# Graph network, third edge stage: inverse square roots for four batches together in place of eight, and every later step four iterations closer to the gathers

## The reference, cut to what matters

```python
row, col = (edge_index[0], edge_index[1])
msg_in = jnp.concatenate([x[row], edge_attr], axis=-1)
h = msg_in @ W1 + b1
h = jax.nn.gelu(_layernorm(h, g1, be1), approximate=False)
msg = h @ W2 + b2
agg = jax.ops.segment_sum(msg, col, num_segments=x.shape[0])
```

## Time and profile before

| what | value |
|---|---|
| median of 3 runs | 5689.45 us (5686.22 to 5690.82) |
| the profiled execution, its own time | 5686.47 us |
| its span, first to last instruction | 5684.7 us |
| DVE busy | 4391.6 us (77%) |
| PE busy | 4194.4 us (74%) |
| POOL busy | 4193.2 us (74%) |
| ACT busy | 3617.8 us (64%) |
| mean granted TensorE clock | 0.846 of full |
| third edge stage, first gather to the start of the next stage | 3679.09 to 4709.18 us |

### The profile page before, as it was taken

The page is one execution under the profiler, slowest core; times in us unless marked ns, Lnnn a source line. Parts: engine busy times, 40 slices in busy tenths (PEclk is TensorE's granted clock), DMA queues, the critical chain, the costliest instruction groups (busy, mean ns, idle before and its releaser), DMA issues.

```text
span 5684.7 us, 86448 instructions
## 1 busy us (share of the span) xinstructions
PE 4194.4 (74%) x23301; PEld 3144.9 (55%) x23378; DVE 4391.6 (77%) x13886; ACT 3617.8 (64%) x12260; POOL 4193.2 (74%) x3819
## 2 busy tenths in 40 slices
PE   4766666766666666675688888578888885999995
PEld 3666665666666656565455555345555554554553
DVE  5887878787878787785788888667777776777776
ACT  4776767676767676673577777356776763555552
POOL 4787887788878787786577777577777754777776
PEclk6877777777777777777899999779999997999997
DMA  8867676767676766664477666456666662555553
GB/s 258 176 161 191 162 177 161 175 163 177 162 177 161 175 163 168 168 162 83 136 200 199 196 199 197 135 179 214 213 209 210 212 186 70 160 155 160 159 159 107
DMA packets 629401, 977.07 MB, mean 172 GB/s; under 512 B 105688, under 2 KB 339026, under 8 KB 628642
## 3 DMA queue, kind: packets, MB, share of 16 engines
q1 hardware_dynamic: 394242, 616.02, 33.7%
q0 software_dynamic: 234656, 355.35, 29.6%
HBM read 668.28 MB, written 306.11 MB: 171 GB/s over the span
## 4 chain that ended last, share of the span: by engine, by line
POOL 52%; issue 22%; DMA 12%; PE 8%; DVE 5%; ACT 1%; POOLq 0%; SPq 0%; DVEq 0%; ACTq 0%
POOL arena L1539 28%; POOL tab L1185 12%; POOL arena L1203 10%; DMA tab<-arena 9%; DMA arena<-T,srcI 2%; POOL arena L1236 1%; PE PS L1702 1%; PE PS L2043 1%; PE PS L2021 1%; PE PS L1497 1%; POOL arena L1209 0%; PE PS L828 0%; PE PS L301 0%; PE PS L848 0%; DVE arena L1526 0%
## 5 line engine op out<-in xcount | busy, mean ns | idle before, releaser
L1539 POOL DMA_INDIRECT arena<-T,srcI x2112 | 2022.0, 957 | 779.4 <-issue 632.1
L1185 POOL DMA_INDIRECT tab<-arena x784 | 1243.2, 1586 | 282.4 <-issue 223.7
L1203 POOL DMA_INDIRECT arena<-T,srcI x784 | 789.5, 1007 | 285.4 <-issue 275.0
L1526 DVE TENSOR_TENSOR_SCAN arena<-arena,PS 128x512 f32<-128x512 bf16 x588 | 748.3, 1273 | 180.9 <-PE PS L2348 81.3
L1506 ACT ACTIVATE arena<-PS 128x512 f32<-128x512 f32 x588 | 347.8, 591 | 640.8 <-PE PS L1497 640.8
L867 PE MATMUL PS<-arena 128*128 128x128 f32 x1568 | 306.2, 356 | 542.1 <-ACT arena L1132 542.1
L1606 DVE TENSOR_SCALAR arena<-PS,nodeid 128x512 bf16<-128x512 f32 x908 | 627.0, 737 | 75.5 <-PE PS L1587 75.4
L867 PEld LDWEIGHTS PS<-arena 128*128 128x128 f32 x1568 | 263.5, 254 | 581.0 <-ACT arena L1132 581.0
L848 PE MATMUL PS<-We,arena 65*128 65x256 f32 x1568 | 510.0, 408 | 58.1 <-DVE arena L890 31.7
L1702 PE MATMUL PS<-arena 128*128 128x396 bf16 x2800 | 541.8, 351 | 8.3 <-DVE arena L1606 6.8
L2330 PE MATMUL PS<-arena 128*128 128x512 bf16 x2323 | 543.8, 381 | 4.2 <-issue 0.2
(11 more groups left out here) (301 smaller groups left out, 10643.6 us busy)
## 6 DMA issues: line engine op xcount, KB each, us to landing
H<-arena SPq DMA_DIRECT2D x784, 256.0 KB, 2.3
arena<-keepR SPq DMA_DIRECT2D x294, 256.0 KB, 5.3
arena<-sF SPq DMA_DIRECT2D x98, 512.0 KB, 6.2
arena<-wF SPq DMA_DIRECT2D x98, 512.0 KB, 7.1
arena<-dF SPq DMA_DIRECT2D x98, 512.0 KB, 8.6
arena<-T,srcI POOLq DMA_INDIRECT x2896, 3.2
arena<-in_ea64T SPq DMA_DIRECT2D x98, 256.0 KB
arena<-S SPq DMA_DIRECT2D x98, 256.0 KB
```

Of the source, the lines that this page charges most:

```text
L1185: e.indirect_dma_start(out=tabs[k % KT], out_offset=at_rows(iA[b % 10][:, c:c + 1]), in_=X2[b % 3][:, c, :], in_offset=None, compute_op=AL ...
L1203: e.indirect_dma_start(out=Gs[b % NR][:, c, :], out_offset=None, in_=T0, in_offset=at_rows(srcI[:, CB * b + c:CB * b + c + 1])).then_inc(g ...
L1526: ins = e.tensor_tensor_scan(s[b % n][:, h, :], kR[g % 6][:, h0:h0 + CB * P], src[h], s[(b - 1) % n][:, h, CB * P - 1:CB * P] if b else in ...
L1539: e.indirect_dma_start(out=dst[:, c, :], out_offset=None, in_=T_tab, in_offset=at_rows(srcI[:, CB * b + c:CB * b + c + 1])).then_inc(gs.of ...
```

## The change

The group of batches for which the chain is run shrinks from eight to four: the tiles `var`, `rst`, `root`, `nh_` and `na_` go from 32 to 16 columns, the chain runs 49 times in place of 25, and each has the same 13 instructions. Since a group is now full after four batches, all steps from D on move four iterations forward: D from offset 12 to 8, T and r from 13 to 9, W from 14 to 10, the scan from 15 to 11, B, the copy and the store from 16 to 12, and SP's load of flags from 8 to 4. The loops end after `NBAT + 12` iterations. The gathers, the ring of 14 buffers, C, t and sq keep their place.

```diff
-            C8 = 8 * CB
-            NQ8 = (NBAT + 7) // 8
+            CQ = 4 * CB
+            NQ4 = (NBAT + 3) // 4
...
-                for i in range(NBAT + 16):
+                for i in range(NBAT + 12):
...
-                    if 0 <= i - 8 < NBAT and i % 2 == 0:
-                        rows_load(e, i - 8, kR, keepR, ld_k, scan)
-                    if 0 <= i - 16 < NBAT:
-                        back_sp(e, i - 16, H2, Ob, O_, so)
+                    if 0 <= i - 4 < NBAT and i % 2 == 0:
+                        rows_load(e, i - 4, kR, keepR, ld_k, scan)
+                    if 0 <= i - 12 < NBAT:
+                        back_sp(e, i - 12, H2, Ob, O_, so)
...
-                    if 0 <= i - 13 < NBAT:
-                        pe_T(e, i - 13)
+                    if 0 <= i - 9 < NBAT:
+                        pe_T(e, i - 9)
...
-                    if 0 <= i - 14 < NBAT:
-                        pe_W(e, i - 14)
-                    if 0 <= i - 16 < NBAT:
-                        back_pe(e, i - 16, 1, [bank(6)], s1, scan, B, O_)
+                    if 0 <= i - 10 < NBAT:
+                        pe_W(e, i - 10)
+                    if 0 <= i - 12 < NBAT:
+                        back_pe(e, i - 12, 1, [bank(6)], s1, scan, B, O_)
...
-                    b = i - 15
+                    b = i - 11
...
-                    if 0 <= i - 4 < NBAT and ((i - 4) % 8 == 7 or i - 4 == NBAT - 1):
-                        dve_rstd8(e, i - 4)
-                    if 0 <= i - 12 < NBAT:
-                        dve_D(e, i - 12)
+                    if 0 <= i - 4 < NBAT and ((i - 4) % 4 == 3 or i - 4 == NBAT - 1):
+                        dve_rstd4(e, i - 4)
+                    if 0 <= i - 8 < NBAT:
+                        dve_D(e, i - 8)
...
-                    if 0 <= i - 13 < NBAT:
-                        act_r(e, i - 13)
-                    if 0 <= i - 16 < NBAT:
-                        back_act(e, i - 16, [bank(6)], Ob, B, O_, so)
+                    if 0 <= i - 9 < NBAT:
+                        act_r(e, i - 9)
+                    if 0 <= i - 12 < NBAT:
+                        back_act(e, i - 12, [bank(6)], Ob, B, O_, so)
```

24 lines of the change are left out of this document (12 added, 12 removed).

## The result

| | before | after |
|---|---|---|
| median | 5689.42 us of 10 runs (5681.0 to 5696.96) | 5669.76 us of 10 runs (5658.5 to 5674.05) |
| ratio after / before, 95% interval | | 0.997 (0.9961 to 0.998) |
| profiled execution, its own time | 5686.47 us | 5673.5 us |
| its span | 5684.7 us | 5671.8 us |
| third edge stage | 1030.09 us | 1016.27 us |

The kernel is faster by 0.3%. The median lies 7.5 us under the forecast and 1.2 us under the low end of its range. The interval of the ratio stands for 11 to 22 us of gain on 5689.42. The forecast's 12.1 us is inside it.

The account below looks back on a forecast made before the run. The prediction took the stage to be paced by POOL's gathers, then a tail; only the tail's 4 x 3.03 = 12.1 us counted, other terms 0. So 5689.45 - 12.1 = 5677.3 us median, range 5671 to 5684 for 8 in 10.

Parts of the forecast that it names:

- The tail: After the stage's last gather: loops end four iterations sooner, 3.03 us each, so 12.1 us less.
- The half-clock stretch: In the tail's long first iteration, W takes 3.34 us instead of 1.72; falling elsewhere, it gives back or costs 1.6 us.
- The chain itself: On the tail once: a chain of 16 columns costs the same as 32 within 0.1 us, so 0.
- The 24 more chains: On DVE between scan and D: 62.4 us more, covered by 218.3 us of waiting for gathers, so 0.
- such a case at 20.46: In the loop, four iterations with the longest chain iteration: 8.70 + 3 x 3.92 = 20.46 us, giving a time of 5700.
- Other waits: 0: On DVE, the chain's wait for sq, 7.6 us in 10 of 25 cases, comes twice as often under cover: 0.
- The ring: T frees gather buffers four iterations (20 us) sooner, but nobody waits: 0; rival that it helps, 3%, 5671.8.
- the filling of the pipeline: At the start of the stage, filling the pipeline lies under the gathers: 0.
- Part of the tail given back: Rival, 10%: in the tail PE stays at half clock two or three more iterations, 1.6 us each: 5680 to 5682.
- The loop falls behind: Rival, 6%: four iterations with one chain outlast the gathers' supply, deciding from 20.25 us; likely 5702 to 5707.
- POOL held by the chains: Rival, 3%: each chain holds one gather, 1 us giving 5701, at most 5740; decides from 0.50 us a chain.
- other sign: In the next stage one gather takes 5.21 us beside DVE's work, so something there holds POOL.

Follow-up runs that it names:

- groups of three: Against the changed kernel, groups of three batches with D at offset 6 and later steps two iterations closer, 66 chains: 5679.56 us, 0.9999 of the kernel before.
- The chain twice: The changed kernel with the inverse square root's 12 instructions run a second time and a copy between them: 5821.0 us, 1.0251 of the kernel before.
- Groups of two: Against the changed kernel, groups of two batches, D at offset 6, later steps two iterations closer, chain ahead of D: 5723.18 us, 1.0071 of the kernel before.
- the experiment: Changed kernel plus a 128x256 DVE copy per iteration, SBUF to SBUF, then PSUM to SBUF: 6291.65 us, 1.0033, where the kernel before took 6269.25.
- both that cut the circle: Two variants of groups of two: one puts the chain behind D (0.996 of the kernel before), one puts sq first on ACT (0.9963).
- the chain behind D: Groups of two with only DVE's order changed, D ahead of the chain, 98 chains: 5657.48 us, 0.996 of the kernel before.
- sq first: Groups of two with only ACT's order changed, sq ahead of r and the copy out: 5665.88 us, 0.9963 of the kernel before.

## Why the prediction was right, and where its numbers were off

**The tail: right.** Four iterations of 3.03 us were to drop out and did. Putting the old offsets back under groups of four takes the gain away; one iteration less gives 2.8 us more by the tail, with the half-clock stretch taken off. Two iterations less give 6.06 us by the stage, a figure that other terms happen to leave intact.

**The half-clock stretch: the term of 1.6 us, with its sign open.** It fell on the good side: W behind the last chain at 1.72 us. It is chance rather than effect, since the kernel with D one iteration sooner has such a stretch again, which costs 1.7 us, and the kernel with the old offsets has none. Of the forecast's stage, 1030.1 - 12.1 = 1018.0, the measured 1016.27 differs by this nearly alone.

**The chain itself: a little cheaper than forecast.** The prediction set 2.37 us without the first instruction beside 2.61 with it and called the two the same within 0.1. Compared alike, from the chain's first instruction to the next one behind it, the median over the stage is 2.77 us for 32 columns and 2.55 for 16. The forecast's 0 should have been -0.2; the last chain shows 2.61 and 2.45.

**The 24 more chains: right that they are free, and a sum that is right at full clock by two errors that cancel.** I had put four iterations with one chain at 18.0 us of the 20.0 supplied, from 6.28 for the one with a chain and 3.92 for each other. Under pressure and at full clock, groups of three show 7.58 us with the chain, since the wait for sq is then in it nearly every time, and 3.43 and 3.51 without. Four such iterations would take 7.58 + 3.43 + 2 x 3.51 = 18.0 us, an estimate with the forecast's sum and other terms. With one half-clock stretch (1.6 us) in every four it would be 19.6. The prediction had such a case at 20.46, from the longest iteration, and it was right to keep it as a price. The chain twice, less a second chain of 2.6, gives 20.6 as an upper estimate, with 6.0 us of half clock in it. In the changed kernel itself three of 47 sets of four iterations have no wait for a gather at all, and they take 17.12, 18.39 and 20.15 us. So the slack is near 2 us at full clock and can be none with half clock. The loop does not need it: 157.6 us of waiting over 49 groups is 3.2 us in every four iterations, and the lag at the last gather is 4.7 us (4660.74 to 4665.46, where t of that batch begins), as in the kernel before (4.8).

**"Other waits: 0": right for this change, wrong in kind.** I named the wait for sq, saw that it was 7.6 us in 10 cases, and costed it at nothing because DVE had cover. At four batches that holds. But I also called it a wait for the batch just squared. It is the one for the batch of the iteration before, which ACT could have squared long ago had it not stood behind a copy that waits for B. A wait inside a loop of engines is not a fixed cost under a cover; it is there whenever the cover is not.

**The ring, SP, the filling of the pipeline: 0, right.** POOL's waits for T have the length of the issue gap in both.

**The rivals.** Part of the tail given back: no, the five iterations at the end run at full clock. The loop falls behind: not here, but real one step further, and from the point given (20.25 us for four) it is not far. The likely cause given for it, iterations at half clock, is what tips groups of three. Groups of two fall behind at full clock too, through the wait for sq. POOL held by the chains: no, 741.4 us for the gathers.

The Trainium skill (SBUF — State Buffer, "SBUF: two separate sides") says that VectorE and GpSimd take their shared ports by an exclusive lock, and that whichever starts first gets it while the other blocks. The copies of the experiment agree with it in both directions: copies that start late in a gather are held, and three gathers that start just behind a copy take up to 1.08 us. But only copies that start 0.55 to 0.70 us into a gather are held, so the gather does not keep the ports for its whole length, and the mean stays at 946 ns.

The prediction's other sign, one gather of 5.21 us in the next stage, is there again at 4.42 us. DVE runs one line back to back beside it; before:

```profile
4726.71 5.86 DVE L1314 SCALAR_TENSOR_TENSOR arena<-vec,deg,arena 128x128 f32<-128x128 f32 x22
```

The gather ends at 4733.38, which is 0.82 us after the last instruction of this row, and the distance is 0.81 or 0.82 us in all ten profiles outside the slow chip. It is the distance of the three gathers that a copy held. So this work of DVE very likely holds POOL, though no run takes it away. The small instructions of the chain do not, on average: the gathers' 741.4 us are those of before.

The clock over 860 us of the stage (busy PE, PEld, DVE, ACT, POOL, clock, DMA share, GB/s), before, changed, and with 98 chains behind D:

```profile
3780.00:4640.00 860.00, 721.80 (x4131) 491.44 (x4130) 654.99 (x790) 610.42 (x1902) 650.36 (x689) 0.96 0.69 212
```

```profile
3780.00:4640.00 860.00, 723.98 (x4130) 488.59 (x4129) 699.13 (x1075) 609.71 (x1893) 650.40 (x689) 0.97 0.69 212
```

```profile
3780.00:4640.00 860.00, 708.92 (x4129) 484.25 (x4128) 780.10 (x1635) 605.07 (x1892) 650.39 (x689) 0.98 0.69 212
```

DVE takes on 44 and 125 us more, and the granted clock does not fall: 0.96, 0.97, 0.98. The Trainium skill (TensorE: Matmul & The Clock Gate, "A second HAM failure mode: psum-queue depth-cycling") tells of another kernel in which frequent short idles of TensorE between groups of matmuls make the clock swing between its levels. The changed kernel and both that cut the circle do not bear that out (0.97 to 0.99). Groups of three do swing, between windows of 1.00 and 0.89, and the chain twice, whose pauses are not short, has 0.87.

**The size of the total.** The change is worth about 12 to 14 us: 12.1 by the four iterations, 13.8 by the stage with a half-clock stretch less, 13.4 by the medians of the repeated measurement. The 19.7 of the first measurement has an interval of 11 to 22, and its surplus is in no stage that the change touches. The low end of the range, 5671, allowed 2 to 3 us for the runs. That was too little for the comparison of two kernels, when the end of the first edge stage alone moves by 18 us between profiles and the kernel before has medians from 5675.43 to 5689.42 us on the chips used.

**What stays open.** Whether the chain behind D and sq first together gain more; it was not tried. What decides whether a group gets a half-clock stretch. Why one chip needs 6269 us. What moves the end of the first edge stage.

The fastest version is groups of two with the chain behind D: 5657.48 us, 0.996 of the kernel before. Against the changed kernel it was not measured side by side; by the stage it is 6.06 us shorter.

## What to carry to other kernels

Where a stage is paced by its first step, what its depth costs is the tail: the number of iterations between the last gather and the last store, times an iteration of what is left in them. Here that was 3.03 us for each iteration taken away, as long as the loop, pressed, took less than the step that paces it.

Measure the pressed loop on iterations with no wait for the pacing step, because waits that circle through several engines (here chain, D, T, B, copy, sq) show in full only there. Then split these iterations by granted clock before you average: here groups of three hold at full clock (14.52 us of 15.0) and fail only by half-clock stretches, while groups of two fail at full clock as well (10.46 of 10.0). For the second kind, look for the one place in the order of an engine where the circle can be cut.

## What the runs showed of the hardware that was not expected

- A DVE copy of 128x256 from SBUF to SBUF beside POOL's gathers takes 284 ns at best and up to 516, by where in the gather it starts. A gather that starts just behind such a copy takes up to 1.08 us instead of 0.945. I had expected the delay, if there was one, on POOL's side alone.
- A gather that DVE holds ends 0.82 us after DVE lets go: three gathers beside copies, and the gather of 3.9 to 5.7 us beside L1314 in each of ten profiles.
- What a chain costs hangs mostly on the number of instructions that depend on each other and little on their width. From its first instruction to the next one behind it, the median of 13 instructions is 2.77 us for 32 columns, 2.55 for 16 and 2.44 to 2.48 for 8.
- One half-clock stretch of 3.4 us costs 1.6 us of the loop in groups of three (16.10 us against 14.52), the same as in the tail.
- The same kernel has medians of 5675 to 5689 us in four measurements and of 6269 us on one further chip.
